# Three of eight input terms u·B of a state-space scan made on TensorE with diagonals of B, one expert input instead of two, and the expert matmuls in another order

## What is computed

```python
def step(state, inp):                       # the Mamba scan, over the tokens
    x_t, dt_t, B_t, C_t = inp
    dA = jnp.exp(dt_t[:, :, None] * A[None])
    state = state * dA + (dt_t * x_t)[:, :, None] * B_t[:, None, :]
    y_t = jnp.einsum('bds,bs->bd', state, C_t)
    return (state, y_t)

def _experts_mlp(x, g, W1, b1, W2, b2):     # 8 routed and 2 shared experts, H = 512
    xn = _rmsnorm(x, g)                     # x * rsqrt(mean(x*x) + eps) * g
    h = jax.nn.gelu(jnp.einsum('btc,ech->bteh', xn, W1) + b1, approximate=False)
    return jnp.einsum('bteh,ehc->btec', h, W2) + b2
```

## Time and profile before

| | |
|---|---|
| median of 3 runs | 2091.42 us (2090.21 to 2092.62) |
| span of the profiled execution | 2094.4 us |
| first scan, last scan start | 241.0 us, 2074.3 us |
| ordinary group (not a head) | 27.93 us, all alike |
| head groups, in turn | 34.6 and 31.8 us |
| first group of all | 37.6 us |
| PE, DVE, ACT, POOL busy | 70%, 96%, 57%, 70% |
| mean granted clock of TensorE | 0.961 of full speed |

### The profile page before, as it was taken

The page is one execution under the profiler, slowest core; times in us unless marked ns, Lnnn a source line. Parts: engine busy times, 40 slices in busy tenths (PEclk is TensorE's granted clock), DMA queues, the critical chain, the costliest instruction groups (busy, mean ns, idle before and its releaser), DMA issues.

```text
span 2094.4 us, 31007 instructions
## 1 busy us (share of the span) xinstructions
PE 1462.3 (70%) x5912; PEld 443.6 (21%) x5912; DVE 2002.3 (96%) x2364; ACT 1202.6 (57%) x1660; POOL 1469.2 (70%) x662
## 2 busy tenths in 40 slices
PE   1678576667666776777666776677666776676666
PEld 1422111112111221122121211122111221121111
DVE  6798699999999999999999999999999999999997
ACT  1477676555566655556555566555566655565551
POOL 4110178876888777787787788877888787778785
PEclk9778799999999999999999999999999999999999
DMA  3134554465444644464445544464445544554442
GB/s 77 68 118 146 155 131 105 110 141 115 115 100 106 165 103 106 110 145 109 115 106 132 135 99 104 112 159 100 114 99 136 135 104 104 128 126 111 115 110 72
DMA packets 179964, 243.06 MB, mean 116 GB/s; under 512 B 17786, under 2 KB 78212, under 8 KB 179780
## 3 DMA queue, kind: packets, MB, share of 16 engines
q1 hardware_dynamic: 179948, 242.89, 47.5%
HBM read 219.13 MB, written 23.20 MB: 116 GB/s over the span
## 4 chain that ended last, share of the span: by engine, by line
issue 40%; DVE 24%; PE 17%; ACT 12%; ACTq 2%; DVEq 2%; SPq 1%; DMA 1%; POOL 1%; POOLq 0%
DVE ps L798 15%; ACT arena L586 9%; PE ps L927 6%; DVE arena L805 4%; PE ps L982 3%; PE ps L877 2%; PE ps L939 1%; PE ps L956 1%; ACTq L586 1%; PE ps L947 1%; DVE arena L814 1%; PE ps L1011 1%; SPq L223 1%; ACTq L583 1%; DVEq L797 1%
## 5 line engine op out<-in xcount | busy, mean ns | idle before, releaser
L447 POOL TENSOR_TENSOR arena<-arena 128x1024 f32<-128x1024 f32 x512 | 1205.0, 2358 | 526.8 <-DVE arena L805 387.5
L805 DVE TENSOR_TENSOR_SCAN arena<-arena,ps 128x512 f32<-128x512 f32 x1024 | 1202.8, 1228 | 6.1 <-POOL arena L447 4.3
L586 ACT ACTIVATE arena<-arena,neg_A 128x512 f32 (+1 forms) x1024 | 661.3, 712 | 205.5 <-DVE arena L805 203.7
L798 DVE TENSOR_TENSOR ps<-arena,ps 128x512 f32<-128x512 f32 x1024 | 666.1, 710 | 3.2 <-PE ps L927 3.2
L927 PE MATMUL ps<-b_parts,pick 96*128 (+1 forms) x512 | 200.6, 392 | 478.3 <-DVE ps L798 473.6
L939 PE MATMUL ps<-arena,ident 64*64 64x512 f32 x3584 | 498.5, 627 | 31.7 <-PE ps L982 25.3
L601 ACT ACTIVATE arena<-ps,b1r_sb 128x512 f32<-128x512 f32 x256 | 175.0, 687 | 366.9 <-PE ps L982 365.4
L982 PE MATMUL ps<-x_rms_routed,arena 128*128 (+1 forms) x512 | 277.3, 623 | 6.2 <-DMA arena<-w_shared_tiles 6.1
L927 PEld LDWEIGHTS ps<-b_parts,pick 96*128 (+1 forms) x512 | 49.3, 96 | 917.6 <-issue 869.1
L1011 PE MATMUL ps<-arena 128*128 128x512 f32 x512 | 242.7, 596 | 0.0
L939 PEld LDWEIGHTS ps<-arena,ident 64*64 64x64 f32 x3584 | 96.2, 133 | 344.0 <-issue 344.0
(11 more groups left out here) (121 smaller groups left out, 759.4 us busy)
## 6 DMA issues: line engine op xcount, KB each, us to landing
arena<-c_scratch SPq DMA_DIRECT2D x128, 1024.0 KB, 8.8
arena<-in_L_ffn_W_r_dram SPq DMA_DIRECT2D x128, 256.0 KB, 8.4
arena<-gate_scratch SPq DMA_DIRECT2D x64, 256.0 KB, 8.7
arena<-w_shared_tiles SPq DMA_DIRECT2D x128, 64.0 KB, 8.6
arena<-dt_scratch SPq DMA_DIRECT2D x9, 512.0 KB, 8.3
arena<-u_scratch SPq DMA_DIRECT2D x9, 512.0 KB, 9.2
sz_scratch<-arena SPq DMA_DIRECT2D x8, 512.0 KB, 4.4
xs_scratch<-arena SPq DMA_DIRECT2D x8, 512.0 KB, 2.9
```

Source lines behind the costliest of these rows:

```text
L447: nc.gpsimd.tensor_tensor(products[:, i % RING, :, :], states[:, i % 2, :, :], c_rows[:, i // CG, i % CG, :].unsqueeze(1).broadcast_to((P, ...
L586: nc.scalar.activation(decay[:, 2 * i + h, :], dflat[:, ds(slot + h * L, L)], ACT.Exp, scale=aflat[:, ds(col, 1)]).then_inc(s["decay_ready ...
L798: vector.tensor_tensor(u_b[h][:], uflat[:, ds(slot + h * L, L)], b_bc[:], ALU.mult).then_inc(s["u_b_multiplied"], 1)
L805: vector.tensor_tensor_scan(states[:, i % 2, h, :], decay[:, m, :], u_b[h][:], 0.0, ALU.mult, ALU.add).then_inc(s["scanned"], 1)
```

## The change

1. The 8 states of a group are of two kinds, `"DEDDEDDE"`. For a D state DVE multiplies as before, but in another bank plan: the three banks ps0 to ps2 rotate, B arrives in the one that is free, and the products are written over the bank of the scan just ended and over B itself. For an E state (1, 4 and 7) DVE multiplies nothing: PE writes u·B into both banks (`fill`), as a matmul of u turned (tokens in partitions) with a 128x128 diagonal of B for each 128 tokens. A fill of one half is 8 float32 matmuls of 64x128, for the two halves of the array's columns in turn.
2. For that, ACT makes the four diagonals of each E state (L677, `ident` times a column of B turned), right after the state's two decays: 12 instructions of 128x128 a group. Once a block, PE turns the next block's u in steps 3 and 5 of the last group (two times four transposes), and ACT copies it out.
3. B of the E states is projected turned in the preparation (8 small matmuls and one ACT copy a block); B of the D states is projected together with C in one product (104 columns), and its bf16 parts need 3 DMAs a block and not 6.
4. The norm weights of the experts are multiplied into W1 instead of the input: W1 is loaded to SBUF at the start, scaled by POOL (one instruction of 128x4096, one of 128x1024), and stored to DRAM scratch. One expert input is kept, and DVE copies it once (8 instructions, not 16).
5. PE does hidden tiles 0 and 1 of the next group in steps 6 and 7, tile 2 in step 0, tiles 3 and 4 in step 1; the W2 tiles come in steps 2, 3, 4, 5 and 7. SP's loads of a group are ordered to suit: W1, first half of the C rows, W2, gate, shared W2, second half of the C rows; before, it was C, W1, C, W2, gate. The W1 load waits for the hidden tiles of the group before, the W2 load for its expert sum.
6. PE's and ACT's code is written out for odd and even blocks, and on PE for the last group.

```diff
+    KIND = "DEDDEDDE"
...
+                    if KIND[i] == "D":
+                        k = D_AT.index(i)
+                        new = second if first == held else first
...
+                        for bank in (held, new):
+                            h = 0 if bank == first else 1
+                            vector.tensor_tensor(ps[bank][:], uflat[:, ds(slot + h * L, L)], ps[new][:],
+                                                 ALU.mult).then_inc(s["u_b_multiplied"], 1)
...
+                    if i in E_AT:
+                        e = E_AT.index(i)
+                        at = snap(b * (SE * TPB) + g * (NE * TPB) + e * TPB)
+                        for c in range(TPB):
+                            ins = nc.scalar.activation(b_diag[:, e, c, :], ident[:], ACT.Copy,
+                                                       scale=bt_flat[:, ds(at + c, 1)])
+                        ins.then_inc(s["diag_ready"], 1)
...
+            def fill(n, i, u, odd, h):
...
+                if h == 0:
+                    pe.wait_ge(s["scanned"], n * 2 + (SCANS - 2))
+                    pe.wait_ge(s["diag_ready"], u * NE + (e + 1))
+                else:
+                    pe.wait_ge(s["scanned"], n * 2 + (SCANS - 1))
+                bank = ps[BANKS[i][h]]
+                for c in range(TPB):
+                    for r in range(2):
+                        ins = mm(bank[HP * r:HP * r + HP, c * P:(c + 1) * P],
+                                 u_turned[:, odd, c, h * P + HP * r:h * P + HP * r + HP], b_diag[:, e, c, :],
+                                 start=True, stop=True, skip_group_check=True)
...
+            W1_AT = {0: (2,), 1: (3, 4)}
+            W1_NEXT_AT = {6: (0,), 7: (1,)}
+            W2_AT = {2: (0,), 3: (1,), 4: (2,), 5: (3,), 7: (4,)}
...
+            def hidden_tile(u, t, t0):
+                if t == 0:
+                    pe.wait_ge(s["w1_loaded"], u * 32 + 32)
+                if t == 1:
+                    pe.wait_ge(s["expert_gated"], u + 1)
+                pe.wait_ge(s["gelu_ready"], u * (HT + 1) + (max(t - 1, 0) + 1))
...
-                for dst, g in ((x_rr, g_routed_col), (x_rs, g_shared_col)):
-                    ins = vector.tensor_scalar(dst[:, b * L:(b + 1) * L], ps[(2 * b + 1) % 8][:], g, None, ALU.mult)
-                ins.then_inc(s["expert_inputs_made"], 1)
+                vector.tensor_copy(x_rms[:, b * L:(b + 1) * L], ps[(2 * b + 1) % 8][:]
+                                   ).then_inc(s["expert_inputs_made"], 1)
```

More of the change, by code:

```diff
@@ L42, in mamba_gated_moe, with bank_plan @@
     CG = SG // 2
+    KIND = "DEDDEDDE"
+    D_AT = [i for i in range(SG) if KIND[i] == "D"]
+    E_AT = [i for i in range(SG) if KIND[i] == "E"]
+    ND, NE = len(D_AT), len(E_AT)
+    SD, SE = E * ND, E * NE
+    NQ = 1 if 3 * SD <= P else 2
+    SQ = SD // NQ
+    def bank_plan(straight):
+        first, second, free = 0, 1, 2
+        plan = []
+        for i in range(SG):
+            if i in straight:
+                first, second, free = free, first, second
+            else:
+                first, second, free = first, free, second
+            plan.append((first, second, free))
+        return plan if (first, second, free) == (0, 1, 2) else None
+    BANKS = next(plan for r in range(ND + 1) for extra in itertools.combinations(D_AT, r)
+                 for plan in [bank_plan(set(E_AT) | set(extra))] if plan)
     ctx = ExitStack()
@@ L255, in store_bc @@
                 for k in range(3):
-                    for q in range(2):
+                    for q in range(NQ):
                         sp.dma_start(b_parts[k * SQ:(k + 1) * SQ, q, ds(t0, L)],
@@ L610, in run @@
                 act.wait_ge(s["dt_u_loaded"], b * 32 + 32)
-                group(b, 0, slot, last, first=last is None)
+                group(b, 0, slot, last, first=last is None, head=True)
                 with act.Fori(1, E) as g:
@@ L1021, in group, with run @@
                         add_to_y(RING)
-            def run(b, last):
+                    if ahead and KIND[ahead[1]] == "E":
+                        fill(*ahead, ahead_odd, 1)
+            def run(b, odd, last):
                 t0 = snap(b * L)
-                group(b, 0, t0, last, head=True)
-                with pe.Fori(1, E) as g:
-                    group(b, g, t0)
-            run(0, None)
+                after = snap((b + 1) * L) if not isinstance(b, int) or b + 1 < NB else None
+                group(b, 0, odd, t0, t0, last, head=True)
+                with pe.Fori(1, E - 1) as g:
+                    group(b, g, odd, t0, t0)
+                group(b, E - 1, odd, t0, after)
+            turn_u(0, 0, 0)
+            pe.wait_ge(s["ut_copied"], 1)
+            turn_u(0, 0, 1)
+            bcast(0, 0, 0, 0, 0)
+            pe.wait_ge(s["ut_copied"], 2)
+            for t in (0, 1):
+                hidden_tile(0, t, 0)
+            run(0, 0, None)
             pe.wait_ge(s["b_c_dt_u_stored"], 16 * N_SDT * (NB + 1))
-            with pe.Fori(1, NB) as b:
-                run(b, b - 1)
+            for b, odd in turns(pe):
+                run(b, odd, b - 1)
             for i in range(-LAG, 0):
```

262 lines of the change are left out of this document (178 added, 84 removed).

## The result

The changed kernel takes **2163.61 us**, median of 4 runs (2161.35 to 2171.19); the kernel before took 2090.82 us beside it. The ratio is 1.037, 95% interval 1.034 to 1.040: slower by 3.7%, where the prediction had 2105 us. The profiled execution has a span of 2161.9 us, 67.5 more than before.

A forecast was written before the change was run, and what follows sets the result against it. DVE, busy for 96%, was taken as the bound; ordinary groups -9, heads +21 - 6, last groups +5, first group +3, preparation -0.5 gave +13.5: span 2108, run 2105 us, range 2058 to 2170.

The forecast's parts named there:

- The chain at the start of a group: Diagonals, gelu of tile 0, hidden tile 2, sum, then state 1's second fill: readable at 7.4, DVE waits 2.9 us.
- A fill: 16 records on PE with column halves running at once: 1.07 us until DVE may read, bounds 0.9 and 1.8.
- Heads: Seven head groups, 3.0 us longer each from PE's block-end work before state 4's second fill: +21, less 6 for half clock.
- last groups: Last group of each block: turning u on PE adds 0.7 us, seven times, +5.
- the sum of the ordinary group: Removed multiplications save 3.57 us, waits at states 1 and 4 add 2.9 and 0.5: 27.75, -9 us over 49 groups.
- The clock, a term put at nothing: PE's half clock was counted in head groups only, -6 us there; ordinary groups got no term for it.
- the fill of state 4: Its second fill, readable at 16.9, makes DVE wait 0.4 us in ordinary groups, entered as 0.5.
- longer fills, 2145 to 2200: Rival: a fill on PE takes 1.15 to 1.4 us; chance 0.11.
- POOL or a DMA holds it: Rival: POOL, with 1.4 us to spare at 24.4 a group, or a DMA sets the time, about 2120 us; chance 0.03.
- The chain is shorter: Rival: with faster diagonals and releases DVE loses only 0.5 to 1 us a group, 2045 to 2075 us; chance 0.16.
- what the removed multiplications give is given back here: DVE's 2.9 us wait at state 1's second scan, in every group, set against the 3.57 saved.
- the preparation: Work before the first group: fewer copies and DMAs against turning B and u and scaling W1, sum -0.5 us.

The follow-up runs named there:

- e7: Changed kernel, but in each fill the eight matmuls of the left column half come before the eight of the right: 2221.3 us, ratio 1.064 to the kernel before.
- e1: Changed kernel with seven more, unneeded copies of B made by PE in its wait for the gelu of tile 0: 2116.7 us, ratio 1.015 to the kernel before.
- e4: Changed kernel without half of the fill matmuls of states 4 and 7, so its output is wrong: 2155.7 us, ratio 1.034 to the kernel before.
- e5: Changed kernel with the old order of PE's expert matmuls and of SP's loads, E states kept: 1960.9 us, ratio 0.937 to the kernel before.
- e3: Changed kernel with ACT making the diagonals of state 7 behind the group's five gelus: 2077.8 us, ratio 0.995 to the kernel before.
- e2: Changed kernel with state 1's second fill right behind its first, ahead of hidden tile 2 and the sum: 2045.5 us, ratio 0.980 to the kernel before.
- e9: Changed kernel with PE's old order of expert matmuls, but SP's loads in the new order: 1960.5 us, ratio 0.939 to the kernel before.
- e11: Changed kernel with all eight states D, plus extra copies of B on PE ahead of its waits in non-head groups: 2114.4 us, ratio 1.013 to the kernel before.
- e6: Changed kernel with all eight states D, no fills or diagonals, new order kept: 2118.0 us, ratio 1.014 to the kernel before.

## Why the prediction was off

**Right, with their sizes.** The chain at the start of a group: forecast readable at t = 7.4; in the rows above the fill ends at 342.83, that is t = 342.83 - 335.44 = 7.39. The gelu of tile 0 ends at 338.93 + 0.69 - 335.44 = 4.18, as forecast. (335.44 is t = 0, the multiplications of state 0.) The second scan of state 1 starts 2.8 us late (forecast 2.9), that of state 4 0.36 (worked out as 0.4, entered in the sum as 0.5). A fill is 1.09 (forecast 1.07). The Trainium skill's page TensorE: Matmul & The Clock Gate, Part 3, The mechanism, by which the loads of a fill should show because all its matmuls use the same rows, does not describe these fills: 16 records with 16 loads take 1.09 us; e7 shows that a pace of 0.1 a record comes back when the column halves don't alternate.

**Right in the sum by luck.** Heads and last groups hold within 1 us, but not by the forecast's terms.

*Heads, +15.6 against +15.* I had put 3.5 us of extra wait at the second fill of state 4. DVE waits 0.07 there, and 3.6 earlier, at three reads of the block's end (changed kernel, head of block 2):

```profile
731.28 1.29 DVE L857 TENSOR_TENSOR arena<-ps,arena 128x512 f32<-128x512 f32 x2 [1.60 <-PE ps L1081]
733.22 0.69 DVE L861 TENSOR_TENSOR arena<-ps,arena 128x512 f32<-128x512 f32 x1 [0.65 <-PE ps L1084]
...
738.67 0.69 DVE L865 TENSOR_TENSOR arena<-ps,arena 128x512 f32<-128x512 f32 x1 [1.32 <-PE ps L1090]
```

And a head at full clock grew by 3.4, not 3.0 (24 us and not 21 over seven), while only one of them is long by half clock now, so that 8 us came back, not 6.

*Last groups, +5.4 against +5.* Turning u was to cost 0.7 a group; five of the seven take 28.25, 0.13 more than ordinary ones. The rest is what the ordinary groups also pay, two stretches at half clock among it.

**The step that failed** is the sum of the ordinary group, "An ordinary group: 27.93 - 3.57 + 2.9 + 0.5 = 27.75. There are 49 such: -9 us". Of its terms the 2.9 is right. One term is missing and one is the wrong one.
- *The clock, a term put at nothing.* I wrote of PE's wait for the gelu that it hides nothing, and let the half clock of the earlier trace rows act on head groups alone. But in that wait of 2.1 us PE does nothing, and in 24 of these 49 groups (23 of the 48, and the very last) the clock is granted at 0.50 behind it, on the very sum and fill that DVE waits for: 24 x 1.6 = 38 us. e1 shows it: with the wait filled, no long group is left.
- *POOL, and not the fill of state 4.* The 0.5 for the fill of state 4 adds nothing by itself: e4 takes that wait away, and the group stays at 28.11, because the scan of state 6 waits for POOL's product of state 4 either way. I had left POOL out because its load left 1.4 us to spare; what holds is its chain of product 3, pair and product 4. e5, which has no wait at state 1, gives the size: 25.26 is 0.9 above the 24.36 of the forecast, some 0.7 of it at the scan of state 6 and 0.13 ahead of the scans of state 2, which start 0.72 behind the second multiplication and not 0.59 as those of states 0, 3 and 5. So 0.9 stands in place of 0.5, and 25.26 + 2.86 (the wait at state 1 by the distance of the scans) is the 28.12 of the short groups, 0.37 more than forecast: 18 us over 49 groups.

Together 56 us, which is the difference between -9 and +47.

**The rivals.** That the kernel would be slower had the larger chance, but its named mechanism (longer fills, 2145 to 2200) was the wrong one; the time fell into that range, and into the stated 2058 to 2170, by the clock and POOL. "POOL or a DMA holds it" had a chance of 0.03, and POOL does hold a part. "The chain is shorter" did not happen by itself; e3 and e2 made it happen, and gave 2078 and 2046, about the values of that rival.

**What the forecast did not ask.** It took the change as one thing. The step "what the removed multiplications give is given back here" names the place (hidden tile 2 ahead of the second fill), and e5 and e9 show that the place was made by part 5 alone, by PE's order. Had I costed the E states against the old order, where tile 2 comes two steps after gelu 0, the wait at state 1 would have been absent.

**Not settled:** the preparation. Its forecast of -0.5 fits, but the first scan starts between 232.4 and 240.8 us in the runs above that share this preparation, so it is not tested. Nor is it settled what made the heads longer (see e11).

## What to carry to other kernels

When a bound engine is relieved and another takes over its work, read the queue of the new engine at the place where its product is wanted: one instruction with a late operand ahead of the wanted one can cost much of what was gained (118 us in e2, where only the fill moved ahead of it; 203 for the whole order), and a reordering made beside it has to be costed apart. Cost an engine with time to spare by its chain too, not by its load alone: here POOL, busy for 69%, holds a scan in every ordinary group. A wait of TensorE inside a chain is paid twice when the clock drops behind it (2.1 us and then 1.6 here): read the granted clock behind each such wait, and fill the wait if it can't be removed. Issue small matmuls with the column halves alternating; here that takes 3 us of TensorE's work, and 1.6 us of time, out of each group.

## What the hardware showed that I had not expected

- Half clock behind a wait of 1.8 to 2.1 us in 26 of the 56 groups of the changed kernel that are not heads, with PE busy for 85% of the span; behind waits of 1.27 us in each of those groups of e3, none.
- A wait is not the only thing ahead of such a fall: in the head of the earlier trace rows PE had been busy without a gap from 477.7 until the granted clock went from 1.00 to 0.50 at 485.2.
- Whether half clock costs time depends on who waits: 26 stretches on the chain cost 41 us; between e6 at a clock of 0.891 and e11 at 0.955 the ordinary and last groups differ by 11 us in all.
- 16 matmuls of 64x128 in float32 with 16 weight loads take 1.09 us with the halves alternating and 1.58 with one half behind the other.
